# A second attention layer's first round: work for a round ahead that does not exist, and who casts the weights

## The reference, cut to what matters

```python
def _L1_xattn_ref(z1ss, u1ss, Wqkv0, Wqkv1, Winj0, Winj1, Wo, bo, r_w_bias):
    # 16 heads of 64; z1ss is the first layer's result, u1ss the context
    for i in range(2):                      # the two halves of the columns
        h = einsum('od,bdl->bol', Wq_list[i], z1ss[:, :, s:e])
        h = h + einsum('od,bdl->bol', Wi_list[i], u1ss[:, :, s:e])
    ...
    q, k, v = split(w_heads, 3, axis=1)
    score = einsum('bndi,bndj->bnij', q + r_w_bias, k) * SCALE
    prob = softmax(score, axis=-1)
    attn_vec = einsum('bnij,bndj->bndi', prob, v)
    attn_out = einsum('od,bdl->bol', Wo, attn_vec) + bo
    x = attn_out + z1ss
    m = mean(x, axis=1); var = var(x, axis=1)
    return (x - m) * rsqrt(var + LN_EPS)
```

## Time and profile before

| | |
|---|---|
| median of three runs | 1244.78 us (1242.97 to 1244.86) |
| the profiled execution | 1244.36 us, its span 1242.4 us, mean TensorE clock 0.99 |
| TensorE, VectorE, ScalarE, GpSimd busy | 95%, 73%, 65%, 45% of the span |
| round 0 of the second layer, steps 0 to 7 | 469 to 558 us |
| DMA over the span | 25.38 MB, mean 20 GB/s |

### The profile page before, as it was taken

One profiled execution on the slowest core, in us unless ns is written; L12 is line 12 of the kernel. 1 busy time (PEld: TensorE's weight loads), 2 busy tenths in 40 slices (PEclk: granted clock), 3 DMA queues, 4 the chain that ended last, 5 costly groups with the idle time before them and its releaser, 6 DMA issues.

```text
span 1242.4 us, 29741 instructions
## 1 busy us (share of the span) xinstructions
PE 1178.3 (95%) x10914; PEld 991.5 (80%) x10914; DVE 904.6 (73%) x1772; ACT 813.7 (65%) x2443; POOL 560.8 (45%) x551
## 2 busy tenths in 40 slices
PE   4799999999999888999999999999999999999998
PEld 3677787887877667788888888888888888888675
DVE  4778989889897757766667666666766766676564
ACT  3587978889787747566665565666665655666443
POOL 3455656555453427643333434333334334334343
PEclk8899999999999999999999999999999999999999
DMA  3260000000000000000000000000000100000011
GB/s 105 71 247 19 14 15 18 13 12 9 15 10 6 1 0 27 2 10 1 1 11 1 2 9 2 2 10 1 10 2 2 56 2 1 1 2 2 18 44 43
DMA packets 18590, 25.38 MB, mean 20 GB/s; under 512 B 1440, under 2 KB 17056, under 8 KB 17952
## 3 DMA queue, kind: packets, MB, share of 16 engines
q1 hardware_dynamic: 18464, 23.69, 5.7%
HBM read 21.58 MB, written 2.10 MB: 19 GB/s over the span
## 4 chain that ended last, share of the span: by engine, by line
PE 59%; DVE 1%; ACT 1%; issue 1%; DVEq 0%; SPq 0%; ACTq 0%
PE psum L1859 15%; PE psum L1911 9%; PE psum L1894 9%; PE psum L1878 8%; PE psum L1861 7%; PE psum L1921 4%; PE psum L1340 1%; PE psum L1406 1%; ACT prob L2015 1%; PE psum L1354 1%; PE psum L1945 1%; PE psum L1930 1%; PE psum L1937 1%; PE psum L1382 1%; PE psum L1364 0%
## 5 line engine op out<-in xcount | busy, mean ns | idle before, releaser
L1793 POOL TENSOR_TENSOR prob<-prob,l_z_inv 128x512 f32<-128x512 f32 x256 | 263.5, 1040 | 383.6 <-DVE l_z_inv L2118 383.5
L2015 ACT ACTIVATE prob<-psum,l_neg_max 128x256 f32<-128x256 f32 x512 | 238.5, 480 | 204.0 <-DVE l_neg_max L2111 204.0
L794 ACT ACTIVATE ring_e<-ring_e,neg_max 128x128 f32<-128x128 f32 x512 | 164.3, 406 | 15.0 <-DVE neg_max L973 14.9
L2111 DVE TENSOR_REDUCE l_neg_max<-psum 128x2 f32<-128x512 f32 x256 | 158.6, 681 | 10.8 <-PE psum L1878 10.8
L1894 PE MATMUL psum<-ident,prob 128*128 128x128 f32 x1024 | 134.0, 274 | 5.8 <-ACT prob L2015 5.8
L1894 PEld LDWEIGHTS psum<-ident,prob 128*128 128x128 f32 x1024 | 117.3, 142 | 16.5 <-issue 7.2
L478 POOL TENSOR_TENSOR ring_e<-ring_e,cross_add 128x512 f32<-128x512 f32 x64 | 85.2, 1348 | 93.2 <-DVE ring_e L968 93.2
L1911 PE MATMUL psum<-pT,vs 128*64 128x256 f32 x1024 | 124.7, 386 | 0.0
L478 POOL TENSOR_TENSOR ring_e<-ring_e,self_add 128x512 f32<-128x512 f32 x64 | 85.9, 1356 | 62.6 <-DVE ring_e L968 61.9
L2015 ACT ACTIVATION_READ_ACCUMULATOR prob<-psum,l_neg_max 128x1 f32 x512 | 107.9, 211 | 0.0
L2142 DVE SCALAR_TENSOR_TENSOR kl<-psum,kh 128x512 fp32r<-128x512 f32 x64 | 44.2, 691 | 87.4 <-ACT kh L2037 87.4
(11 more groups left out here) (213 smaller groups left out, 3220.5 us busy)
## 6 DMA issues: line engine op xcount, KB each, us to landing
wz_raw<-wz_in SPq DMA_DIRECT2D x2, 1536.0 KB, 15.1
wi_raw<-wi_in SPq DMA_DIRECT2D x2, 1536.0 KB, 19.8
x_in<-x SPq DMA_DIRECT2D x8, 256.0 KB, 2.7
cT<-ctxT SPq DMA_DIRECT2D x8, 256.0 KB, 2.8
w<-w_in SPq DMA_DIRECT2D x2, 1024.0 KB, 9.4
l_ub<-ctx_in SPq DMA_DIRECT2D x8, 256.0 KB, 2.7
cg<-ctx_in SPq DMA_DIRECT2D x4, 512.0 KB, 3.9
out<-fin SPq DMA_DIRECT2D x7, 256.0 KB, 2.1
```

The lines of the kernel that those rows point to most:

```text
L794: last = nc.scalar.activation(e, e, ACT.Exp, bias=neg_max[:, n % RE, h:h + 1])
L1793: pool.tensor_tensor(e, e, z_inv[:, t % RE, h, :].unsqueeze(2).broadcast_to([P, 2, D]), ALU.mult)\
L2015: last = nc.scalar.activation(prob[:, t % RE, h, qt * D:(qt + 1) * D], score_bank[b][h][:, qt * D:(qt + 1) * D], ACT.Exp, bias=neg_max[:, ...
L2111: nc.vector.tensor_reduce(neg_max[:, t % RE, h, :], score_bank[b][h].rearrange("p (t c) -> p t c", t=2), AX.X, ALU.max, negate=True).then_ ...
```

## The change

It does two things in the second layer. First, in round 0 the four products of the normalisation, `centre`, `read_variance`, `inverse_std`, `make_diagonal`, `output` and the clearing of `y` are not done. In the place of each of the four products TensorE waits for the bank and issues a nop that counts as the filling, and VectorE waits for that and issues a nop that counts as the reading; SyncE's first nops give `y_done`, `squared`, `rstd_done` and `diagonal` the credit of one round more. Second, `IN_TURN` gives the parts to other steps, and part 2 (`v1`, `ALL_BY_ACT`) is cast by ScalarE for all four tensors. The semaphores of the casts are named by engine, and `hi_later` finds the count to wait for.

```diff
-        IN_TURN = [(2, 3), (4,), (5,), (6,), (7, 8), (9,), (), ()]
+        IN_TURN = [(2, 3), (4,), (5, 6), (7,), (8,), (9,), (), ()]
+        ALL_BY_ACT = 2
...
+        def hi_later(n, m):
+
+            by_act = m < 2 or n == ALL_BY_ACT
+            same = [(k, j) for k in range(AT_ONCE, len(PARTS)) for j in range(len(tensors))
+                    if (j < 2 or k == ALL_BY_ACT) == by_act]
+            return (act_hi_later if by_act else dve_hi_later), same.index((n, m)) + 1
...
         def _(sp):
 
+            done = (zu_hi, zu_lo, y_done, squared, rstd_done, diagonal)
             for e in events:
-                sp.nop().then_inc(e.sem, 2 * e.per if e in (zu_hi, zu_lo) else e.per)
+                sp.nop().then_inc(e.sem, 2 * e.per if e in done else e.per)
...
             def rest_later(n):
                 for m, (hi, lo, raw) in enumerate(tensors):
-                    pool.wait_ge((z_hi_later, i_hi_later)[m // 2], 2 * (n - AT_ONCE) + m % 2 + 1)
+                    pool.wait_ge(*hi_later(n, m))
...
-                    if n == T_READ:
+                    if n == T_READ and not first:
                         inverse_std(i, "var")
...
-            def fill(found):
+            def fill(found, first):
                 for name, r in found:
                     if is_made(name):
                         project(r, name)
+                    elif first:
+                        pe.wait_ge(*work.free(name, r))
+                        pe.nop().then_inc(work.fills(name), 1)
...
             def round_later(n):
-                for hi, lo, raw in tensors[0:2]:
-                    nc.scalar.copy(part(hi, n), part(raw, n)).then_inc(z_hi_later, 1)
+                for m, (hi, lo, raw) in enumerate(tensors):
+                    if m < 2 or n == ALL_BY_ACT:
+                        nc.scalar.copy(part(hi, n), part(raw, n)).then_inc(act_hi_later, 1)
...
             def rests(found, first):
                 for name, r in found:
                     if is_made(name):
                         rest_work(r, name)
+                    elif first:
+                        dve.wait_ge(*work.full(name, r))
+                        dve.nop().then_inc(work.reads(name), 1)
...
                     if first:
                         for m in IN_TURN[n]:
-                            round_later(m)
+                            if m != ALL_BY_ACT:
+                                round_later(m)
...
-                    if n == T_DIAG:
+                    if n == T_DIAG and not first:
                         make_diagonal(i)
...
-            nc.vector.memset(y[:, :, :], 0.0).then_inc(y_done.sem, 1)
```

More of the change, by code:

```diff
@@ L1705, in layers123 @@
             "weights_hi_made", "z_weights_lo_made", "i_weights_lo_made", "wo_hi_made", "wo_lo_made"))
-        z_hi_later, i_hi_later, lo_later = (sem(n) for n in (
-            "z_weights_hi_later", "i_weights_hi_later", "weights_lo_later"))
+        act_hi_later, dve_hi_later, lo_later = (sem(n) for n in (
+            "weights_hi_by_act", "weights_hi_by_dve", "weights_lo_later"))
         FILLS = [("q1", "k1", "v0b1"), ("q2", "k2", "v1b0"), ("q3", "k3", "v1b1", "mean"),
@@ L1966, in body @@
                         times_v(*behind(i, n, 2))
-                    fill(f[0:1])
+                    fill(f[0:1], first)
                     if n >= 1 or not first:
                         turn(*behind(i, n, 1), 0)
-                    fill(f[1:2])
+                    fill(f[1:2], first)
                     if first and n == 2:
@@ L1976, in body @@
                         turn(*behind(i, n, 1), 1)
-                    fill(f[2:])
+                    fill(f[2:], first)
                 if last:
@@ L2184, in make_diagonal, with output @@
                 last.then_inc(diagonal.sem, 1)
-            def output(i, name, b, first=False, bank=work):
+            def output(i, name, b, bank=work):
                 dve.wait_ge(*bank.full(name, i))
                 ps = bank.psum(name)[:, 0:D]
-                to = y[:, b, :] if first else xs[:, bass.ds((i - 1) * NB + b, 1), :].rearrange("p a d -> p (a d)")
+                to = xs[:, bass.ds((i - 1) * NB + b, 1), :].rearrange("p a d -> p (a d)")
                 nc.vector.tensor_tensor(to, y[:, b, :], ps, ALU.mult).then_inc(bank.reads(name), 1)
@@ L2199, in round_later @@
                 for hi, lo, raw in tensors[2:4]:
-                    nc.vector.tensor_copy(part(hi, n), part(raw, n)).then_inc(i_hi_later, 1)
+                    nc.vector.tensor_copy(part(hi, n), part(raw, n)).then_inc(dve_hi_later, 1)
             def rests(found, first):
@@ L2210, in rests @@
                     else:
-                        output(r, name, int(name[3]), first)
+                        output(r, name, int(name[3]))
             def body(i, first, last):
```

## The result

The changed kernel takes 1235.38 us (median of five runs, 1233.08 to 1236.99) against 1244.84 us (1242.97 to 1244.98): ratio 0.9935, interval 0.9922 to 0.9948, so it is faster by 0.65%, clear of the noise. The forecast was 1237.4, in a range of 1235.0 to 1240.5.

The account below looks back on a forecast made before the run. TensorE's path was taken to bound the kernel, with round 0's holes opened by VectorE's queue. Terms: 1.50 + 0.86 + 0.79 + 0.44 + 4.61 - 1.0 - 0.1 = 7.1 us, giving 1237.4 us, range 1235.0 to 1240.5.

Parts of the forecast that it names:

- two casts fewer after step 0: Round 0, step 1: VectorE casts two blocks, not four, so maxima start earlier and TensorE's 1.96 us hole shrinks; gain 1.50.
- `mean`, `var`, `inv0`: Normalisation products in steps 2, 3 and 5 of round 0 leave TensorE's path: gains 0.86, 0.79 and 0.44 us.
- `inv1`: Step 6 of round 0: leaving out this product gains nothing, as `v3b1` waits for VectorE's `kl`; bounds 0 and 0.1.
- the clearing of `y`: Before round 0: dropping VectorE's 0.48 us clearing gains nothing, as the first exponential also waits for ScalarE's rounding of Wo.
- the stall of step 5: Round 0, step 5: with two casts and no diagonal ahead of the maxima, the whole 4.61 us stall goes.
- new stall in step 3: Round 0: four casts after step 2 delay the next maxima, costing 1.0 us, expected 0.8 to 1.3, bounds 0 and 2.0.
- waits and nops: Four pairs replacing the normalisation products in round 0 cost TensorE between 0 and 0.24 us, taken as 0.1.
- free time: Round 0 steps: maxima may start up to 2.42 us after the scores at no cost; each us beyond costs one.
- the two new waits of step 3: Round 0, step 3: two short TensorE waits for exponentials, 1.0 us in all, behind four casts of 2.5 to 3.0 us.
- 1244.36 - 8.1: Rival of no stall in step 3, casts finding gaps in GpSimd's work: 1236.2, down to 1235; chance 0.12.
- The Trainium skill's rule of the port: Two-port VectorE instructions and GpSimd exclude each other for a whole instruction: 0.95 us per cast, sum 6.5.
- The rival with the clock: The stall moves to step 3 and lowers TensorE's clock, costing 1.2 plus up to 1: 1239.2 to 1241.5; chance 0.13.

Follow-up runs that it names:

- casts alone: Kernel before with only the new `IN_TURN`, `ALL_BY_ACT` and `hi_later`, normalisation of round 0 kept: 1238.62 us, ratio 0.9967.
- the swap: Changed kernel with `v3b1` ahead of `inv1` among the fillers of step 6 in every round: 1234.23 us, ratio 0.9920.
- parts 2 and 6 by ScalarE: Changed kernel with part 6 too cast by ScalarE alone, so VectorE has two casts after step 2, not four: 1233.89 us, ratio 0.9928.
- the second: Series that ran the changed kernel again, unaltered, against the kernel before: 1235.08 us against 1242.74, ratio 0.9940.

## Why the prediction was right

Its frame, that the path through round 0 is TensorE's and that VectorE's queue opens its holes, is what the runs show from step 1 on; in step 0 Wo's DMA is a second gate. Term by term, in us:

| step of the prediction | forecast | measured | shown by |
|---|---|---|---|
| two casts fewer after step 0 | 1.50 | 1.50 | step 1 after, and casts alone (1.48) |
| `mean`, `var`, `inv0` | 2.09 | 0.86 + 0.78 + 0.44 | steps 2, 3 and 5 |
| `inv1` | 0 | 0.00 | step 6; its cause by the swap |
| the clearing of `y` | 0 | 0.26 | step 0 after, and casts alone |
| the stall of step 5 | 4.61 | 4.60 | step 5 before and after |
| new stall in step 3 | -1.0 | -0.88 | parts 2 and 6 by ScalarE |
| waits and nops | -0.1 | 0.00 | plain steps of 10.44 to 10.45 |
| sum | 7.1 | 7.57 | |

Three terms were mis-sized. The clearing of `y` was costed at nothing because ScalarE's rounding of Wo covered it. In the profile before the two gates were less than 0.1 us apart (the first exponential starts 0.99 us after that rounding, and 0.95 after it where only the rounding held it), and the rounding hangs on a DMA that landed after 4.1 to 6.1 us in the eleven profiles that issue it behind the nops. The gain of 0.26 needed both the clearing gone and a landing after 4.5 us instead of 4.9. The new stall was sized with a free time of 2.42 and casts of 2.54 to 3.00; they took 2.55 and the free time is 2.29. The nops cost nothing that shows.

Three readings of the prediction were off without moving its sum. It put the maxima of step 5 2.15 us after the scores; they came at 1.70, since the two casts took 1.07 us and not 1.50. It said that the two new waits of step 3 would be 1.0 us in all; the trace lists 0.46, and the step is 0.88 longer. And it read 3.44 us of the stall of step 5 as waiting and 1.17 as slower work, where the trace has 3.06 and 1.54. Among the rivals, 1244.36 - 8.1 is 1236.3 and not 1236.2, and 1.2 to 2.2 us on top of 1237.4 give 1238.6 to 1239.6, not 1239.2 to 1241.5.

The Trainium skill's rule of the port (SBUF — State Buffer, "SBUF: two separate sides") was weighed there with 0.95 us for each cast beside a GpSimd subtraction. Four such casts took 2.55 us, 0.64 each, so that cost was too high here. That VectorE's work takes longer beside the subtractions shows most clearly in the diagonal, 2.82 us under subtractions throughout and 1.83 where they end in its midst. No run here separates the port from another cause.

The median came out at 1235.4 against the 1237.4 forecast. Of these 2.0 us the terms above explain 0.5. The rest is scatter: the two medians of the first series are 9.46 us apart, those of the second 7.66, and the change inside the trace is 7.57. One execution is up to 4 us ahead of another before the second layer begins, so that the number fell inside a range whose lower end is 1235.0 is partly luck; that round 0 lost 7.57 us where 7.1 was forecast is not. The rival with the clock did not come: the two new waits are 0.28 and 0.18 us, and the granted clock of every window of 3 us from 463 to 550 us is 1.00 after the change.

Of the halves, leaving out the normalisation alone takes step 5 from 15.49 to 11.33 us; 0.44 of that is `inv0`, so 3.72 of the stall go. The casts alone take 3.42. Either takes most of the stall, since what is left is only what exceeds the free time. Their gains must not be added.

## What to carry to other kernels

For an engine that has to deliver once per step, work out from one undisturbed step how late it may begin at no cost. Work ahead of it costs only what exceeds that, one for one, so cutting a long queue pays once, and moving work into another step is free until the same limit. Taking a product off the path gives nothing where the next one waits for its bank to be read: look at who reads the bank, and whether another order would do. And a cost of zero that rests on a second gate equally late can turn into a cost in the next execution.

## What the runs showed of the hardware

The same four products on VectorE took 2.82 us with GpSimd's subtractions beside them throughout and 1.83 where the subtractions ended in their midst. Four casts took 2.54 to 3.00 us beside them and 1.98 where GpSimd stood idle for the first two. A pair of casts took 0.48 with GpSimd idle and 1.07 to 1.51 beside it.

The landing of the same 512 KB transfer took from 4.1 to 6.1 us in the eleven profiles in which it is issued behind SyncE's nops, and 3.9 in the two in which it stands ahead of them. Issuing it took SyncE 0.37 us.

The mean granted clock of the first 100 us was 0.91 in eleven of the thirteen profiles, 0.93 in one and 0.97 in one, with the same instructions. After the 2.60 us hole of the kernel before, the clock was 0.62 in the mean from 528 to 532 us, and 0.50, the 1.2 GHz level, from 529 to 532; after the 1.96 us hole and all shorter ones of round 0 it stayed at its full level.
